# FFN layers in six full groups of 8 sequences and nine mixed tiles of 2, in place of ten groups, with a weight ring of four slots and resident gamma and beta

## The chip, the cores and the metric

The kernel runs on one core of one Trainium2 chip. The metric is the device time of one execution in microseconds, lower is better. The time before is the median of three runs.

## What is computed

Four layers over 64 sequences of 64 tokens and 512 features (float32). Layers 0, 2 and 3 are feed-forward layers whose weights are chosen per sequence by a role. The roles drawn are 1 or 2; the kernel has room for three. Layer 1 is attention with two wide feed-forward stages; the change doesn't touch its arithmetic.

```python
# x: [64, 64, 512]; role: [64]; W_down: [3, 512, 256]; W_up: [3, 256, 512]; gamma, beta: [3, 512]
def ffn(role, x, W_down, b_down, W_up, b_up, gamma, beta):
    h = gelu(einsum('bsh,bhk->bsk', x, W_down[role]) + b_down[role][:, None, :])
    y = x + einsum('bsk,bkh->bsh', h, W_up[role]) + b_up[role][:, None, :]
    yn = (y - mean(y)) * rsqrt(var(y) + 1e-5)
    return yn * gamma[role][:, None, :] + beta[role][:, None, :]

x = ffn(role, x, ...)          # layer 0
x = attention_and_mlps(x, ...) # layer 1
x = ffn(role, x, ...)          # layer 2
x = ffn(role, x, ...)          # layer 3
```

## The kernel before

**Grouping.** Sequences are sorted by role on the chip. A group holds 8 sequences of one role, that is 512 tokens or four tiles of 128. Each role starts a new group, so `NG` = 64 / 8 + 3 - 1 = 10 groups cover every possible mix of roles, and 16 of their 80 slots are empty (they are computed all the same). Class `Route` works out the slots: `dve_tables` (L176) is a chain of 49 small DVE steps, each waiting for the one before; PE's `pe_tables` and `pe_ranks` (L260, L270) turn them into row numbers, between the `fold` products (L1010, plain fp32) that prepare matrices for layer 1. POOL copies the numbers into one tile per group (`pool_rows`).

**Precision.** An FFN product is three fp32r matmuls: high x high, high x low, low x high (`product`, L57 to L59). ACT writes the high part (a Copy to fp32r), DVE the low part (a subtraction). This goes for weights (`act_split_down` L469, `dve_split_down` L519), transposed tokens (L486, L538) and hidden values (L497, L545).

**A group.** Class `Ffn` runs layer 0 as `first` (10 groups) and layers 2 and 3 together as `last` (20 groups, `NJ`). POOL gathers a group's rows (L626, one indirect DMA of 128 rows of 8 KB). PE transposes them (16 transposes of 128x128, L423), does the down product (24 matmuls of 512 columns, two banks), ACT the gelu and the split, then PE the up product (4 tiles x 7 matmuls of 512 columns, L455 to L459). DVE adds the residual (L551) and takes statistics (L555, L562), ACT turns them into moments (L504, L505), POOL takes the power -0.5 (L601, L603), ACT normalises (L511), POOL applies gamma (L611) and beta (L616) and scatters the rows (L639). Layer 3 takes its tokens from layer 2's tiles on chip.

**Order.** The order on each engine is written out by hand. On PE, in round j: down product of j, first up tile of j - 1, transposes of j + 1, the other three up tiles of j - 1. On DVE: weight split of j + 1, two hidden parts of j, residual, transposed half, residual, transposed half of j + 1, then statistics and residuals of j - 1. On POOL, in the first layer: gather j + 2, rstd of j - 2, gamma and beta of j - 3, scatter j - 3. ACT's normalisation of j - 2 stands before its transposed half of j + 1.

**Loads.** SP loads a group's down weights (512 KB) into one of two raw buffers `w_raw` when the split of the group two before is done, and gamma and beta (512 KB, broadcast to all partitions, `sp_load_gain` L400) into one of two buffers when the group two before has been shifted. All up weights of a layer stay on chip. The raw buffers are the same that layer 1 uses for its weights.

**Between the stages.** Layer 1 reads its tokens in quarters of 16 sequences from DRAM (`load_x`), once the scatters that hold them have landed. ACT waits for the scatters of groups whose tiles layer 1 overwrites (L1114 and L1124 are its first writes there). At the end the last three groups' gamma and beta are applied by DVE (L569, L572) while POOL does one half tile.

Of the kernel before, what the change touches and what calls it, by code (L numbers as in the profile page):

```python
# [16 lines left out]
F32 = mybir.dt.float32  # L17
# [34 lines left out]

def product(pe, out, terms):
# [29 lines left out]
class Route:  # L83


    ROLES_OUT = 5
    SLOT_OUT = 20
    ROLE_ROW = 26
    FIRST_ROWS = 29
    RANK_OUT = 36  # L90
    CODES_OUT = 39
    TABLES = 45
    ALL = 49

    def __init__(self, nc, ctx, consts, roles, codes, cb2, at, bank):
        self.consts, self.roles, self.codes, self.cb2 = consts, roles, codes, cb2
        tiles = Tiles(nc, at)
# [7 lines left out]
        self.up_i = tiles.new("up_i", [NSEQ, ROLES], I32)  # L105
        self.up_r = tiles.new("up_r", [NSEQ, ROLES], I32)
        self.base = tiles.new("base", [NSEQ, ROLES])
        self.packed = tiles.new("packed", [NSEQ, ROLES])
        self.place = tiles.new("place", [NSEQ, ROLES])
        self.placed = tiles.new("placed", [NSEQ, ROLES])  # L110
        self.slot = tiles.new("slot", [NSEQ, 1])
        self.slot_i = tiles.new("slot_i", [NSEQ, 1], I32)
        self.in_group_i = tiles.new("in_group_i", [NSEQ, 1], I32)
        self.in_group = tiles.new("in_group", [NSEQ, 1])
        self.group = tiles.new("group", [NSEQ, 1])
        self.seq_off = tiles.new("seq_off", [NSEQ, 1])
        self.value = tiles.new("value", [NSEQ, 1])
        self.rank = tiles.new("rank", [NSEQ, 1])
        self.rank_off = tiles.new("rank_off", [NSEQ, 1])
# [3 lines left out]
        self.iota_grp = tiles.new("iota_grp", [NSEQ, NG])  # L123
        self.at_group = tiles.new("at_group", [NSEQ, NG])
        self.rank_at_group = tiles.new("rank_at_group", [NSEQ, NG])
        self.slot_rows = tiles.new("slot_rows", [P, NG])
        self.rows = tiles.new("rows", [P, NG])
        self.rank_rows = tiles.new("rank_rows", [P, NG])
        self.live_rows = tiles.new("live_rows", [P, NG])
        self.past1 = tiles.new("past1", [1, NG])  # L130
        self.past2 = tiles.new("past2", [1, NG])
        self.role_at = tiles.new("role_at", [1, NG])
# [21 lines left out]
        self.coded = sem("coded")  # L154

    def pool_make(self, pool):
# [8 lines left out]
        pool.iota(self.iota_grp[:], pattern=[[GS, NG]], base=0, channel_multiplier=0, **exact).then_inc(made, 1)  # L165
# [3 lines left out]
        pool.iota(self.slot_rows[:], pattern=[[P, NG]], base=NROWS, channel_multiplier=1, **exact).then_inc(made, 1)  # L169
        pool.wait_ge(made, 10)  # L170
# [5 lines left out]
    def dve_tables(self, v, src_row):  # L176
        tab_src, tab_dst, tab_row, target_bias, _ = self.consts
# [7 lines left out]
        step(v.memset(self.base[:], 0.0))  # L185
        step(v.memset(self.packed[:], 0.0))
        v.wait_ge(self.made, 12)
# [8 lines left out]
        step(v.tensor_scalar(self.up_i[:], count, float(GS - 1), None, ALU.add))  # L196
        step(v.tensor_scalar(self.up_r[:], self.up_i[:], -GS, None, ALU.bitwise_and))
        step(v.tensor_copy(self.base[:, 1:2], self.up_r[:, 0:1]))
        step(v.tensor_tensor(self.base[:, 2:3], self.base[:, 1:2], self.up_r[:, 1:2], ALU.add))
        step(v.tensor_tensor(self.place[:], self.base[:], within, ALU.add))  # L200
# [9 lines left out]
        step(v.tensor_scalar(self.at_group[:], self.iota_grp[:], self.group[:], self.value[:], ALU.is_equal, ALU.mult))  # L210
        assert steps[0] == self.SLOT_OUT

        step(v.tensor_scalar(self.past1[:], self.iota_grp[0:1, :], self.base[0:1, 1:2], None, ALU.is_ge))
        step(v.tensor_scalar(self.past2[:], self.iota_grp[0:1, :], self.base[0:1, 2:3], None, ALU.is_ge))
        step(v.tensor_tensor(self.role_at[:], self.past1[:], self.past2[:], ALU.add))
        for layer in range(3):
            step(v.tensor_scalar(tab_row[:, layer * NG:(layer + 1) * NG], self.role_at[:],
                                 float(ROLES * layer), None, ALU.add))
        assert steps[0] == self.ROLE_ROW
        v.wait_ge(self.slots, 1)  # L220
        step(v.scalar_tensor_tensor(out=self.rows[:], in0=self.ps_slot[:, 0:NG], scalar=float(SROWS),
                                    in1=self.slot_rows[:], op0=ALU.mult, op1=ALU.add))
        for j in range(2):
            step(v.tensor_scalar(src_row[j][:], self.rows[:, j:j + 1], float(NROWS - 1), None, ALU.min))
        assert steps[0] == self.FIRST_ROWS

        step(v.tensor_copy(self.packed[:, 1:2], count[:, 0:1]))
        step(v.tensor_tensor(self.packed[:, 2:3], self.packed[:, 1:2], count[:, 1:2], ALU.add))
        step(v.tensor_tensor(self.place[:], self.packed[:], within, ALU.add))
# [1472 lines left out]
```

## Time and profile before

| | |
|---|---|
| three runs | 2487.82 us median (2485.74 to 2488.30) |
| profiled execution | 2487.73 us |
| its span | 2485.9 us, so 1.83 us lie around it |
| mean granted TensorE clock | 0.995 |
| first layer, layer 1, last two layers | to about 185 us, to about 2195 us, to 2485.9 us |
| DMA | 195.32 MB, mean 79 GB/s |
| landing of a 512 KB down-weight load, of a scatter, of a gather (page, median) | 4.5 us, 8.0 us, 9.5 us |

How to read it: times are microseconds from the start of the span unless marked ns. PE is TensorE's matmul row, PEld its weight loads, DVE VectorE, ACT ScalarE, POOL GpSimd, SP SyncE. Matmuls are pipelined: a row's length is the latency of one, and the pace is the distance of the starts. Plain fp32 products have two records each, fp32r products one. A row `PE L423 ... x16` merges sixteen in a row. Idle time of an engine that is not the bottleneck costs nothing.

### The profile page before, as it was taken

Reading aid. Unit: us, or ns where it says so; the run is one execution under the profiler, and the core shown is the slowest. Engines: PE = TensorE matmul, PEld = TensorE weight load, DVE = VectorE, ACT = ScalarE, POOL = GpSimd, SP = SyncE. Lnnn points to the kernel's source line nnn. Section 1 sums busy time; section 2 is a strip of 40 time slices with the busy share of each in tenths; the row PEclk is TensorE's granted clock in tenths of the full one; section 3 lists DMA queues with packets and bytes.
Section 4 is the critical chain, followed back from the end, with each engine's and each line's share of the span. In section 5 each row is a group of like instructions: output and inputs, shape, how many; then the busy total and the mean of one; then the engine's idle time right before and its main releaser. Section 6 shows DMA issues by size and latency. Waiting matters only on the chain.

```text
span 2485.9 us, 27593 instructions
## 1 busy us (share of the span) xinstructions
PE 2445.6 (98%) x11362; PEld 2032.5 (82%) x11362; DVE 1022.3 (41%) x1415; ACT 898.5 (36%) x1227; POOL 402.5 (16%) x312
## 2 busy tenths in 40 slices
PE   8999999999999999999999999999999999999996
PEld 5878888888888888888888888888888888888885
DVE  4774434222333343223243332233433422268776
ACT  4564423222334332223243322232432222346653
POOL 2786000000000000000000000000100000018886
PEclk9999999999999999999999999999999999999998
DMA  6463111210111112111111121102101211144243
GB/s 247 178 219 111 68 51 51 85 51 35 51 68 51 51 51 79 40 51 51 68 52 51 41 78 51 51 28 92 51 34 51 85 51 43 59 163 145 77 144 136
DMA packets 41521, 195.32 MB, mean 79 GB/s; under 512 B 5666, under 2 KB 5666, under 8 KB 24756
## 3 DMA queue, kind: packets, MB, share of 16 engines
q1 hardware_dynamic: 35636, 151.60, 18.0%
q0 software_dynamic: 5760, 41.95, 4.2%
q8 instruction: 91, 1.49, 0.2%
q14 instruction: 34, 0.28, 0.0%
HBM read 162.07 MB, written 31.46 MB: 78 GB/s over the span
## 4 chain that ended last, share of the span: by engine, by line
PE 97%; DVE 1%; DMA 1%; POOL 0%; issue 0%; ACT 0%; SPq 0%; DVEq 0%; ACTq 0%; POOLq 0%
PE pair L57 23%; PE pair L59 23%; PE pair L58 23%; PE pair L962 2%; PE pair L970 2%; PE pair L969 2%; PE pair L961 2%; PE pair L960 2%; PE pair L968 2%; PE pair L459 2%; PE pair L457 2%; PE pair L458 2%; PE pair L423 2%; PE pair L1010 1%; PE pair L937 1%; PE pair L921 1%
## 5 line engine op out<-in xcount | busy, mean ns | idle before, releaser
L1325 DVE TENSOR_TENSOR h_lo<-g,h_hi 128x512 fp32r<-128x512 f32 x256 | 179.1, 700 | 745.1 <-ACT h_hi L1149 744.8
L1147 ACT ACTIVATE g<-pair,bias_cols 128x512 f32<-128x512 f32 x256 | 176.5, 690 | 647.9 <-PE pair L59 411.5
L57 PE MATMUL pair<-h_hi,w_hiB 128*128 128x512 f32 x1024 | 399.0, 390 | 0.0
L59 PE MATMUL pair<-h_hi,w_loB 128*128 128x512 f32 x1024 | 398.4, 389 | 0.0
L58 PE MATMUL pair<-h_lo,w_hiB 128*128 128x512 f32 x1024 | 398.4, 389 | 0.0
L57 PE MATMUL pair<-o_hi,w_hiA 128*128 128x512 f32 x768 | 299.1, 390 | 0.0
L59 PE MATMUL pair<-o_hi,w_loA 128*128 128x512 f32 x768 | 298.8, 389 | 0.0
L58 PE MATMUL pair<-o_lo,w_hiA 128*128 128x512 f32 x768 | 298.7, 389 | 0.0
L1102 ACT ACTIVATE w_hiB<-w_raw 128x2048 fp32r<-128x2048 f32 x36 | 69.1, 1920 | 533.7 <-PE pair L59 504.9
L1537 POOL COPY acc<-xr 128x1024 f32<-128x1024 f32 x16 | 15.9, 1034 | 1357.8 <-PE pair L998 1349.7
L59 PEld LDWEIGHTS pair<-h_hi,w_loB 128*128 128x128 f32 x1024 | 192.2, 188 | 40.0
L58 PEld LDWEIGHTS pair<-h_lo,w_hiB 128*128 128x128 f32 x1024 | 192.3, 188 | 39.8
L57 PEld LDWEIGHTS pair<-h_hi,w_hiB 128*128 128x128 f32 x1024 | 192.2, 188 | 39.4
L59 PEld LDWEIGHTS pair<-o_hi,w_loA 128*128 128x128 f32 x768 | 144.2, 188 | 30.1
L58 PEld LDWEIGHTS pair<-o_lo,w_hiA 128*128 128x128 f32 x768 | 144.2, 188 | 29.8
L57 PEld LDWEIGHTS pair<-o_hi,w_hiA 128*128 128x128 f32 x768 | 144.2, 188 | 29.7
L1149 ACT ACTIVATE h_hi<-g 128x512 fp32r<-128x512 f32 x256 | 162.1, 633 | 8.1
L1332 DVE TENSOR_TENSOR x_tok<-pair,x_tok 128x512 f32<-128x512 f32 x128 | 86.8, 689 | 185.8 <-PE pair L59 185.8
L1332 DVE TENSOR_TENSOR acc<-pair,acc 128x512 f32<-128x512 f32 x128 | 86.0, 687 | 141.9 <-PE pair L59 141.9
L1279 DVE TENSOR_TENSOR w_loA<-w_raw,w_hiA 128x2048 fp32r<-128x2048 f32 x36 | 85.3, 2368 | 67.3 <-ACT w_hiA L1102 67.3
L1279 DVE TENSOR_TENSOR w_loB<-w_raw,w_hiB 128x2048 fp32r<-128x2048 f32 x36 | 84.6, 2350 | 49.1 <-ACT w_hiB L1102 49.1
L960 PE MATMUL pair<-o_hi,w_hiA 128*128 128x512 f32 x256 | 99.6, 389 | 0.0
(234 smaller groups left out, 4370.8 us busy)
## 6 DMA issues: line engine op xcount, KB each, us to landing
w_raw<-in_units_a SPq DMA_DIRECT2D x32, 1024.0 KB
w_raw<-in_units_b SPq DMA_DIRECT2D x32, 1024.0 KB, 4.8
w_raw<-in_units_c SPq DMA_DIRECT2D x16, 1024.0 KB, 4.8
w_raw<-in_w_packed SPq DMA_DIRECT2D x30, 512.0 KB, 4.5
w_raw<-in_rows_packed SPq DMA_DIRECT2D x20, 512.0 KB, 4.5
x<-stage SPq DMA_DIRECT2D x32, 256.0 KB, 2.1
x_tok<-x SPq DMA_DIRECT2D x12, 512.0 KB, 7.5
first_gain<-in_rows_packed SPq DMA_DIRECT2D x10, 512.0 KB, 4.6
```

Source lines behind the costliest of these rows:

```text
L57: pe.matmul(out, lh, rh, start=(i == 0), stop=False)
L58: pe.matmul(out, lh, rl, start=False, stop=False)
L59: last = pe.matmul(out, ll, rh, start=False, stop=(i == len(terms) - 1))
L423: last = pe.transpose(self.turned[i][:, t, k * P:(k + 1) * P], self.x[j % self.NX][:, i * self.HALF + t, k * P:(k + 1) * P], self.consts[4 ...
L457: pe.matmul(self.bank_U[t % 2], self.h_hi[u][:, k, ts], hi[k], start=False, stop=False)
L960: pe.matmul(bank[q], lh, rh, start=(i == 0), stop=False)
L1102: act.activation(w_hi[slot][:].rearrange("p k n -> p (k n)"), w_raw[i], ACT.Copy).then_inc(hi_done[slot], 1)
L1147: act.activation(g[q % 2][:], bank[q % 4], ACT.Gelu, bias=bias_at).then_inc(gelu_done, 1)
L1149: act.activation(h_hi[:, j, cols(n)], g[q % 2][:], ACT.Copy).then_inc(hhi_done, 1)
L1279: v.tensor_tensor(w_lo[slot][:].rearrange("p k n -> p (k n)"), w_raw[i], w_hi[slot][:].bitcast(F32).rearrange("p k n -> p (k n)"), ALU.sub ...
L1325: v.tensor_tensor(h_lo[:, j, cols(n)], g[q % 2][:], h_hi[:, j, cols(n)].bitcast(F32), ALU.subtract).then_inc(hlo_done, 1)
L1332: v.tensor_tensor(into[:, m, cols(n)], bank[4 + r % 4], into[:, m, cols(n)], ALU.add).then_inc(acc_done, 1)
```

## The change

The roles' full groups of 8 are kept, six of them, and every other sequence goes to a tile of two sequences (128 tokens) of one role. Nine such tiles cover every possible mix. Three of them, each with a role of its own, make a mixed job, so a layer is nine jobs, numbered from 0, in the order of `KINDS` (O a full group, M a mixed job), with 33 tiles of 128 tokens in place of 40.

- Mixed jobs: three down weights per job, one for each 128 columns; three gelus of 128 columns per bank; up weights, gamma and beta by tile; three gathers and three scatters of 128 rows of 2 KB.
- Weights: a ring of four slots, whose raw weights land in the place of the low parts and are subtracted in place. A load waits for the down product of the job that used the slot. On DVE and ACT the second and third split of a mixed job are put between the other steps.
- Gamma and beta of all three roles are loaded once per layer; the loads per group are gone. For the third layer they wait until layer 2's up weights are free.
- `dve_tables` has 75 steps in place of 49, with slots, ranks and row numbers for tiles as well.
- The fold matrices are loaded into the raw buffers after the last down product of the first layer (before: after the split of the last group).
- Buffers, and with them the scatters that layer 1 waits for, are placed anew; ACT also waits for the scatters of jobs 5 and 6 before its first values.

```diff
+KINDS = "OOOMOMOOM"
+NP = len(KINDS)
+OCT = KINDS.count("O")
+MT = 3
+MIXED = MT * KINDS.count("M")
+JOBS = tuple((kind == "O", KINDS[:p].count(kind) * (1 if kind == "O" else MT)) for p, kind in enumerate(KINDS))
+T_OF = tuple(GT if octet else MT for octet, _ in JOBS)
+UNITS = tuple((at,) if octet else tuple(OCT + at + i for i in range(MT)) for octet, at in JOBS)
...
-    ROLES_OUT = 5
-    SLOT_OUT = 20
...
-    ALL = 49
+    ROLES_OUT = 6
+    SLOT_OUT = 36
...
+    ALL = 75
...
+    def sp_load_down(self, sp, n):
+        j = self.job_of[n]
...
+        if n >= self.SLOTS:
+            sp.wait_ge(self.down_done, KB * (self.job_of[n - self.SLOTS] + 1))
...
-    def sp_load_gain(self, sp, j):
...
+    def sp_load_gain(self, sp, l):
+        for r in range(ROLES):
+            row = self.layers[l] * ROLES + r
+            sp.dma_start(self.gain[l][:, r, :],
+                         self.rows_packed[row:row + 1, 1:3, :].rearrange("r a n -> r (a n)").broadcast_to([P, 2 * D]))\
+              .then_inc(self.gain_in[l], 16)
...
+        spans = [slice(0, 512)] if octet else [slice(t * P, (t + 1) * P) for t in range(MT)]
         for m in parts:
             if m == 0:
                 pe.wait_ge(self.xlo_done, 2 * j + 2)
-                pe.wait_ge(self.wdlo_done, j + 1)
+                pe.wait_ge(self.wdlo_done, self.UB[j + 1])
...
-            product(pe, self.bank_D[m], [((self.wd_hi[u][:, k, ms], self.wd_lo[u][:, k, ms]),
-                                          (self.xT_hi[:, k, :], self.xT_lo[:, k, :])) for k in range(KD)])\
-                .then_inc(self.down_done, 1)
+            for u, ts in zip(units, spans):
+                last = product(pe, self.bank_D[m][:, ts],
+                               [((self.wd_hi[u][:, k, ms], self.wd_lo[u][:, k, ms]),
+                                 (self.xT_hi[:, k, ts], self.xT_lo[:, k, ts])) for k in range(KD)])
+            last.then_inc(self.down_done, 1)
...
+        for t, ts in enumerate(spans):
+            last = act.activation(self.bank_D[m][:, ts], self.bank_D[m][:, ts], ACT.Gelu,
...
+        else:
+            for t in range(MT):
+                pool.indirect_dma_start(out=self.x[j][:, t, :], out_offset=None, in_=self.src[1][0:TOKENS, :],
+                                        in_offset=bass.IndirectOffsetOnAxis(ap=self.src_rows[j][t][:], axis=0))\
+                    .then_inc(self.x_in[j % 2], 16)
...
+            sp.wait_ge(first.down_done, KB * NP)
+            for f in range(2):
+                sp.wait_ge(fold_stored[f], 16)
+                sp.dma_start(w_raw[f], (fold_m, fold_v)[f]).then_inc(raw_in[f], 16)
...
+            for i in range(2):
+                sp.wait_ge(end_stored[i], 8 * TT)
+            last.sp_load_gain(sp, 0)
...
-            for i in (3, 4):
-                act.wait_ge(first.stored[i], 16 * STORES.count(i))
+            for i in (1, 2, 3):
+                act.wait_ge(first.stored[i], first.stored_all(i))
...
+            for i in (4, 5):
+                act.wait_ge(first.stored[i], first.stored_all(i))
...
                 for m in range(KB):
                     last.dve_hidden(v, j, m)
+                if more:
+                    last.dve_split_down(v, last.units_from(j + 1, 1, 2))
                 last.dve_residual(v, j - 1, 0)
-                if j + 1 < last.NJ:
+                if more:
                     last.dve_transposed(v, j + 1, 0)
                 last.dve_residual(v, j - 1, 1)
-                if j + 1 < last.NJ:
+                if more:
                     last.dve_transposed(v, j + 1, 1)
+                    last.dve_split_down(v, last.units_from(j + 1, 2, 3))
```

## Rows read from the trace of the kernel before

**Rows 1.** Page, part 1: busy time, share of the span, instructions.
```profile
PE 2445.6 (98%) x11362; PEld 2032.5 (82%) x11362; DVE 1022.3 (41%) x1415; ACT 898.5 (36%) x1227; POOL 402.5 (16%) x312
```
**Rows 2.** Page, part 4: the chain that ended last, by engine.
```profile
PE 97%; DVE 1%; DMA 1%; POOL 0%; issue 0%; ACT 0%; SPq 0%; DVEq 0%; ACTq 0%; POOLq 0%
```
**Rows 3.** Chain in order of time (start, us, what): first and seventeenth transposes.
```profile
2220.02 1.75 PE pair L423 x16
...
2436.88 1.75 PE pair L423 x16
```
**Rows 4.** Timeline of PE (start, us, what): a down product's start, the next operation.
```profile
2239.94 0.39 PE L57 MATMUL pair<-last_xT_hi,last_wd_hi 128*128 128x512 f32 x1
...
2245.38 0.39 PE L455 MATMUL pair<-last_up_rows,last_pick 128*128 x1
```
**Rows 5.** Timelines of PE and PEld, then a window: PE, PEld, DVE, ACT, POOL busy, clock.
```profile
2246.97 1.91 PE L423 MATMUL pair<-ident,last_x 128*128 128x128 f32 x16
239.05 7.31 PE L937 MATMUL pair<-probsT,x_tok 128*128 128x128 f32 x64
246.09 0.19 PEld L57 LDWEIGHTS pair<-o_hi,w_hiA 128*128 128x128 f32 x1
246.20 0.19 PEld L58 LDWEIGHTS pair<-o_lo,w_hiA 128*128 128x128 f32 x1
29.09 7.03 PE L1010 MATMUL pair<-factor,factor 128*128 128x512 f32 x16
239.10:246.20 7.10, 7.10 (x67) 7.10 (x65) 4.50 (x6) 5.62 (x9) 0.00 (x0) 1.00 0.00 0
```
**Rows 6.** Timelines of DVE and PE in one steady group; in brackets the idle time.
```profile
2276.43 1.23 DVE L538 TENSOR_TENSOR last_xT_lo<-pair,last_xT_hi 128x1024 fp32r<-128x1024 f32 x1 [1.02 <-ACT last_xT_hi L486]
2278.23 1.21 DVE L538 TENSOR_TENSOR last_xT_lo<-pair,last_xT_hi 128x1024 fp32r<-128x1024 f32 x1
2280.60 0.39 PE L57 MATMUL pair<-last_xT_hi,last_wd_hi 128*128 128x512 f32 x1
2284.32 1.22 DVE L519 TENSOR_TENSOR last_wd_lo<-w_raw,last_wd_hi 128x1024 fp32r<-128x1024 f32 x1
```
**Rows 7.** Timeline of POOL in the first layer: one round and the next gather.
```profile
93.29 0.98 POOL L626 DMA_INDIRECT first_x<-in_x,first_src_row  x1 [0.30 <-issue]
...
95.71 4.73 POOL L611 TENSOR_TENSOR first_x<-first_x,first_gain 128x1024 f32<-128x1024 f32 x2
100.40 4.78 POOL L616 TENSOR_TENSOR first_x<-first_x,first_gain 128x1024 f32<-128x1024 f32 x2
105.47 1.05 POOL L639 DMA_INDIRECT x<-first_x,first_dst_row  x1 [0.29 <-POOL first_x L616]
106.83 0.97 POOL L626 DMA_INDIRECT first_x<-in_x,first_src_row  x1 [0.30 <-issue]
```
**Rows 8.** Timeline of PE at the start: slots, first fold, first transposes.
```profile
8.07 0.60 PE L268 MATMUL pair<-at_group,at_rows 64*128 64x10 f32 x2 [3.17 <-DVE at_group L210]
11.00 5.43 PE L1010 MATMUL pair<-factor,factor 128*128 128x512 f32 x8 [2.33 <-DMA factor<-in_wkT]
...
27.35 1.91 PE L423 MATMUL pair<-ident,first_x 128*128 128x128 f32 x16
```
**Rows 9.** Into layer 1: timeline of ACT and POOL, a stretch's clock, the chain.
```profile
169.01 0.60 ACT L1114 ACTIVATE xr<-pair 128x512 f32<-128x512 f32 x1 [3.46 <-DMA x<-first_x,first_dst_row]
202.13 0.58 ACT L1124 ACTIVATE x_tok<-pair 128x512 f32<-128x512 f32 x1
194.92 1.04 POOL L639 DMA_INDIRECT x<-first_x,first_dst_row  x1 [0.29 <-POOL first_x L616]
176.00:182.00 6.00, 4.71 (x15) 3.58 (x14) 4.52 (x9) 5.78 (x13) 0.13 (x1) 0.72 0.52 198
179.06 0.43 PE pair L457
```
**Rows 10.** Timeline of DVE near the end: gamma for the last group.
```profile
2472.45 2.50 DVE L569 TENSOR_TENSOR last_x<-last_x,w_raw 128x512 f32<-128x512 f32 x4 [0.55 <-DMA w_raw<-in_rows_packed]
```

More of the change, by code:

```diff
@@ L719, in program @@
-        routed = Route(nc, ctx, consts, roles, codes, cb2, where["probs"], bank)
-        assert routed.end <= where["probs"] + 3 * 4 * HT * P
-        folded_at = [first.x[5 + f][:].rearrange("p t n -> p (t n)") for f in range(2)]
+        routed = Route(nc, ctx, consts, roles, codes, cb2, tiles, where["probs"], bank)
+        assert routed.end <= where["probs"] + 3 * 4 * HT * P
+        oct_row, oct_rank = ([(row,) for row in rows] for rows in (routed.oct_row, routed.oct_rank))
+        tok_src, tok_rank, tok_live, tok_dst = (
+            {t: rows[t:t + MT] for t in range(0, MIXED, MT)} for rows in (routed.tok_src, routed.tok_rank, routed.tok_live, routed.tok_dst))
@@ new lines, in per_job, with both_rows @@
+        def per_job(octets, mixed):
+            return [octets[at] if octet else mixed[at] for octet, at in JOBS]
+        def both_rows(a):
+            return a, a.rearrange("a (t n) -> (a t) n", n=D)
+        half = 4 * KD * 512
+        six = 4 * MT * D
+        wd_lo = places["o_hi"] - 2 * half
+        assert wd_lo >= where_raw
+        first = Ffn(nc, ctx, "first", consts, routed, (0,), tiles, {
+            "x": (where["acc"], where["acc"] + half, where["xc_hi"], where["xc_hi"] + half, places["o_hi"],
+                  where["x_tok"], where["x_tok"] + half, places["first_c"], where["h_hi"]),
+            "xT": where["xc_lo"], "h": where["h_lo"], "wd_hi": where["w_hiA"], "wd_lo": wd_lo, "wu": (where["w_hiC"],),
+            "gain": (places["o_lo"],), "raw_rows": places["first_c"], "up_rows": where["h_hi"] + half,
+            "pick": where["h_hi"] + 2 * half - 2048},
+            pairs, both_rows(first_args["src"]), both_rows(first_args["dst"]), per_job(oct_row, tok_src), per_job(oct_rank, tok_rank),
+            first_args["w_packed"], first_args["rows_packed"], STORES)
@@ new lines, in program @@
+        o = places["o_hi"]
+        last = Ffn(nc, ctx, "last", consts, routed, (1, 2), tiles, {
+            "x": (where["x_tok"], where["x_tok"] + half, o, o + half, o + half + six, o + 2 * half + six,
+                  where["acc"], where["acc"] + half, o + 2 * half + 2 * six),
+            "xT": where["xc_hi"], "h": where["h_hi"], "wd_hi": where["xc_lo"], "wd_lo": wd_lo,
+            "wu": (where["w_hiA"], where["w_hiA"] + 8 * ROLES * KB * D), "gain": (where["h_lo"], where["w_hiA"]),
+            "raw_rows": where["probs"], "up_rows": o + 2 * half + 3 * six, "pick": where["expd"]},
+            pairs, both_rows(last_args["src"]), both_rows(last_args["dst"]), per_job(oct_rank, tok_live), per_job(oct_row, tok_dst),
+            last_args["w_packed"], last_args["rows_packed"], [p % 2 for p in range(NP)], first)
@@ L722, in program @@
+        assert o + 2 * half + 4 * six <= places["first_c"] + half
+        folded_at = [sb(f"folded{f}", [P, KD * D], at=where["x_tok"] + half * f) for f in range(2)]
         HIDDEN = HTILES * SB
@@ L851, in _ @@
             sp.wait_ge(lo_done["A"], NA * SB)
[L852 removed]
             sp.wait_ge(lo_done["B"], NBU * SB)
[L854 removed]
+            for n in range(2):
+                last.sp_load_down(sp, n)
             last.sp_load_rows(sp)
@@ L1020, in _ @@
             fold(1, range(2))
-            for j in range(NG):
+            for j in range(NP):
                 first.pe_down(pe, j)
@@ L1163, in _ @@
             act.wait_ge(bias_in, 16)
-            for j in range(NG):
-                role = first.role_of(act, j)
+            for j in range(NP):
+                roles = first.roles_of(act, j)
                 if j >= 2:
```

796 lines of the change are left out of this document (438 added, 358 removed).

## The prediction

> **What bounds the kernel now.** First the page: PE is busy 98% of the span, no other engine over half [rows 1]. A busy PE may still be one that others pace, so next the chain that ended last: 97% of it is PE [rows 2]. The chain in order of time then gives the measure of the stage that the change touches. From 2220.02 to 2436.88 us the transposes of sixteen successive groups come 216.86 us apart, 13.554 us a group, and PE has no wait between [rows 3]. The FFN layers are therefore priced in PE time, and only then does one ask who else could become late.
>
> A group on PE [rows 4]: its 24 down matmuls of 512 columns run from 2239.94 to 2245.38, 5.44 us, 226.7 ns each. (A row's own length, 0.39, is the latency of one; they overlap, so I price by start to start.) The up product has 4 tiles of 7 such matmuls, 28 x 226.7 = 6.35 us. The 16 transposes take what is left, 13.554 - 5.44 - 6.35 = 1.77 us. A layer is ten groups, 135.5 us; three layers, 406.6 us.
>
> **PE's work after.** A layer has six full groups, unchanged: 81.3 us. It has three mixed jobs of three 128-token tiles. Each has 12 transposes (1.32 us) and 3 tiles of up (21 x 226.7 = 4.76 us). The down product can no longer use one weight for 512 columns: each tile has its own, so it is 3 x 24 = 72 matmuls of 128 columns in place of 24 of 512. Columns fall from 512 to 384, instructions triple. The whole case hangs on the pace p of an fp32r matmul of 128 columns with its own weight load, and no such row exists; 3 x 3 x 72 = 648 of them are issued.
>
> Bounds for p. From below: if only columns and the fixed part counted, 226.7 ns for 512 is 213.3 of columns at 2.4 GHz and 13.4 fixed, so 53.3 + 13.4 = 67 ns. From nearby: every 128-column stream of this trace, each with its own weight load, goes at about one pace. The 16 transposes start within 1.91 - 0.27 = 1.64 us, 15 steps, 109 ns; the 64 plain fp32 matmuls of the attention need 7.31 - 0.28 = 7.03 for 63 steps, 112 ns [rows 5]. Two fp32r weight loads that had nothing to wait for start 0.11 us apart (246.09, 246.20) [rows 5]: the load can be had at that pace for this type too. From above: plain fp32 needs two records per product, and a 512-column record takes (7.03 - 0.62)/15 = 427 ns, so a product costs 854 ns, four times the columns. If an fp32r matmul this narrow were run like plain fp32, it would cost 2 x 112 = 223 ns [rows 5]. I take 111 ns, by the transposes and the two loads, and keep 67 and 223 for the range.
>
> Mixed job: 4.76 + 1.32 + 72 x 0.111 = 14.07 us, so slightly more than a full group for three quarters of its tokens. Layer: 81.3 + 42.2 = 123.5 us, 12.0 less. Three layers: -36.0 us.
>
> A rule of the Trainium skill prices this otherwise. "TensorE: Matmul & The Clock Gate", section "Back-to-back issue gap", gives about 81 ns for a stream of 128-column load and matmul pairs. By it the estimate would be 648 x 30 ns = 19 us better than mine. No 4-byte stream here comes under 109 ns, so the trace speaks against it for this type.
>
> **What newly stops PE between jobs.** Before a down product PE waits for DVE's last part of the transposed tokens. In a steady group DVE starts that part at 2278.23, ends it at 2279.44, and PE begins the down product at 2280.60: 1.16 us of slack [rows 6]. The change puts two more weight splits in front on DVE for a mixed job, one before the residuals, one behind the last transposed part. A split is 1.2 us long [rows 6].
> - Jobs 3 and 8 (mixed, behind full ones): the earlier split fits in DVE's idle 1.02 us, the later one eats the slack of 1.16: about 0.2 us each.
> - Job 5 (mixed, two behind mixed job 3): between its transposes and its down product PE has two output tiles of job 3 in place of three, 1.59 us less cover, its own transposes are 0.44 shorter, and the late split adds 1.2; its last part is half as long, -0.6. 1.59 + 0.44 + 1.2 - 0.6 - 1.16 = 1.5, and with the earlier split and the hops between queues 2.
> - Jobs 7 and 10 (full, two behind a mixed one): 1.59 - 1.16 = 0.4.
> - The up tiles that wait for a residual pushed back by a split: 0.5, twice a layer.
> That is 3.5 us a layer, +11 in all; bounds 4 (all of it but job 5's stall fits into jitter) and 25 (every mixed job stalls by 2.8).
>
> POOL is the next suspect: in the first layer it goes round in 13.55 us without rest, gather 1.0, gain and shift 9.4, scatter 1.1, and the rest small operations and 0.3 of issue twice [rows 7]. A mixed job gives it three gathers and three scatters of 1.3 us, +5.3 in all, and takes a quarter of the 9.4, -2.4. The round in which it prepares job 8 and finishes job 3 becomes 16.5 us against 12 of PE; but the layer as a whole has 33 tiles in place of 40, and the rounds ahead leave it some 3 us. What waits for it is ACT's normalisation, which stands ahead of ACT's transposed parts; I count nothing, and up to 6 us in the bound above. In the last two layers gathers and scatters fall into different layers and POOL has rest. ACT's three gelus of 128 columns in place of one are hidden under 6 us of other PE work.
>
> The ring: with four slots a load of 512 KB (4.5 us to land by the page) is issued when the job four units back has left PE, at least one whole job ahead of its use. Nothing. Resident gamma and beta remove twenty-odd loads of 512 KB that nobody but the last two jobs waited for: nothing in the middle.
>
> **The edges.** Start: DVE's table steps come one after another, 15 of them in the 3.17 us that PE waits for the slots, 0.21 each [rows 8], and there are 26 more, 5.5 us. PE stands behind them twice. The slots are 16 steps later, at 11.4 instead of 8.07, and the fold behind them waits for its DMA until 11.00 anyway. The ranks (25 steps later) come near 16.6, when that first fold ends (11.00 + 5.43). The tables must end before PE needs them at 27.35, and do by 6 us [rows 8]. +0.5; bounds 0 and 4 (the folds no longer cover).
> Into the attention: today ACT waits 3.46 us until a scatter has landed, and part of the stretch behind it has a granted clock of 0.72 [rows 9]. After, the same position in the pipeline is scattered (job 4, two rounds before the last), so the wait stays. The fold matrices are now loaded only after the last down product, 5 us before ACT's split asks for them. One scatter more (job 6) must land before ACT copies the first values; at its place POOL today issues a scatter at 194.92, and ACT copies at 202.13 [rows 9], so with a landing of 8 us (the page's median) ACT would be 1 us late, with a whole query product of PE's beside it. +1; bounds 0 and +8.
> Into the last layers: SP waits for the final stores (2 us to land) and issues 1.5 MB of gamma and beta ahead of the second up weights. +1; bounds 0 and +6, when the third and fourth job's weights come late.
> Tail: DVE ends with gains and shifts for ten tiles; one tile less is two operations of 0.61, and the 0.55 us for the last gain load is gone [rows 10]. Against it, the last job has three scatters of 1.3 in place of one [rows 7]. -1; bounds -2 and +2.
>
> **Sum.** 2485.9 - 36.0 + 11 + 0.5 + 1 + 1 - 1 = 2462.4 us of span. The profiled execution took 1.83 us more than its span, and is 0.09 from the median. Forecast 2464.2 us, 0.9% faster. Its own range: p from 109 to 125 ns is -1 to +9, stalls -7 to +14, edges -4 to +16, not all at once: 2452 to 2480.
>
> **Rivals.**
> 1. Narrow fp32r matmuls run four passes, as plain fp32 does. Then p is 223 ns, 648 x 112 = +73 us: 2537 us, slower by 2%. For it: the only 128-column matmuls that multiply here are plain fp32, and the fp32r gain is seen at 512 columns alone. Against it: nothing in the trace links passes to width; 512 and 128 columns of plain fp32 both take two passes a record. It decides from p = 111 + 23.6/0.648 = 147 ns. Chance 0.26. "FP8 and Floating Point Precision", section "TensorE Precision Notes", of the Trainium skill lists four passes for true fp32 and a truncated read for reduced precision, and ties neither to a width; the 854 ns agree with the four.
> 2. The clock falls while the array is half idle for 8 us. The matmuls behind it then go 0.43 us apart instead of 0.227, as at 179.06, inside the stretch with 0.72 [rows 9]. If all 21 up matmuls of nine mixed jobs did, 9 x 21 x 0.2 = +38: 2502 us. Against it: 7.1 us of 128-column stream at 1.00 [rows 5]. Chance 0.05. The skill's "TensorE: Matmul & The Clock Gate", section "Why this matters for your kernels", warns of thin matmuls for this reason and would pad them instead, which is what the kernel before does.
> 3. The cover does not hold: DVE's splits, POOL's sixteen-us round or the late ring loads stall every job at its down product, 27 x 1 us more: 2491 us, within 0.2%. Chance 0.05.
> 4. Loads overlap better, p near 67 ns: 648 x 44 = -28 us, and 4 us more of stalls as covers shrink: 2440 us. Chance 0.06.
> The number of mixed tiles is fixed in the program (15 units whatever the roles), so that PE's work shrinks as stated is certain.
>
> **How the numbers follow.** Forecast 0.58, rivals 0.26, 0.05, 0.05, 0.06. A measurement of this kernel can tell about 0.2%, 5 us. Faster: 0.58 + 0.06 = 0.64. Same: the third, 0.04 after rounding. Slower: 0.26 + 0.05 + 0.01 = 0.32. Fast cases alone hold too little, so the range must reach the first rival: 2450 to 2545, which leaves out rival 4 and some tails.
>
> **What would show it.** Right: 128-column fp32r starts 0.11 us apart in the down product of a mixed job; transposes of two full jobs still 13.55 apart; a wait of about 2 us at job 5 on DVE's weight split, repeated in each layer; the first layer 12 us shorter. Wrong: starts 0.22 apart there (rival 1), a granted clock below 1 behind mixed jobs (2), waits on POOL or DMA at many jobs (3), starts under 0.1 (4).

## The result, and the profile after

The changed kernel takes 2535.97 us (median of four, 2530.98 to 2536.74) beside 2487.45 for the kernel before: a ratio of 1.0192, interval 1.018 to 1.0204. It is 1.9% slower, where 0.9% faster was forecast. The profiled execution took 2530.98 us, the shortest of the four, with a span of 2528.9, so 43.0 us more than the span before. The other three have a mean granted clock of 0.975 beside its 0.977 and are 4.6 to 5.8 us longer; that is about what one more down product at half clock would cost (below), but they were not traced. In what follows L71 to L73 are the down product's matmuls, L523 the transposes, L561 to L565 the up product, L631 DVE's split of a down weight, L651 its last part of the transposed tokens, L665 the residual, L726 and L732 POOL's gain and shift.

The page, part 1, beside [rows 1]: PE is busy 12 us longer though it has less to do, and 71 us of the span are not PE's, 40 before.

```profile
PE 2457.6 (97%) x11493; PEld 2049.7 (81%) x11493; DVE 1023.6 (40%) x1379; ACT 884.1 (35%) x1233; POOL 388.0 (15%) x338
```

The stretches in which the mixed jobs' down products run, eight of the nine (columns: stretch, length, busy PE, PEld, DVE, ACT, POOL, granted clock, DMA share, GB/s). All have the same 72 matmuls.

```profile
78.60:86.67 8.07, 8.07 (x74) 8.07 (x73) 5.42 (x12) 1.85 (x7) 2.91 (x3) 1.00 0.57 207
112.03:127.42 15.39, 15.39 (x73) 15.39 (x73) 4.16 (x9) 1.74 (x6) 13.21 (x9) 0.50 0.38 137
166.77:180.13 13.36, 13.36 (x72) 13.36 (x73) 4.32 (x11) 1.74 (x6) 9.60 (x9) 0.58 0.19 80
2273.78:2288.04 14.26, 14.26 (x72) 14.26 (x73) 4.17 (x9) 1.74 (x6) 11.35 (x7) 0.54 0.22 74
2327.53:2340.99 13.46, 13.46 (x72) 13.46 (x73) 5.42 (x12) 1.75 (x6) 7.41 (x7) 0.58 0.00 0
2391.71:2399.78 8.07, 8.07 (x73) 8.07 (x73) 5.42 (x12) 1.75 (x6) 4.16 (x4) 1.00 0.01 2
2425.12:2440.41 15.29, 15.29 (x72) 15.29 (x73) 4.17 (x9) 1.74 (x6) 12.11 (x8) 0.50 0.17 70
2480.44:2488.51 8.07, 8.07 (x73) 8.07 (x73) 4.32 (x11) 1.74 (x6) 4.44 (x4) 1.00 0.32 133
```

At full clock the product takes 8.07 us, the forecast's 72 x 0.111 = 8.0. In five of nine jobs the mean granted clock is 0.50 to 0.58, so most or all of the time is at the lower level of 1.2 GHz, and the same work takes 13.4 to 15.4. One of these jobs, job 8 of the second layer (timeline of PE), starts at full clock and loses it after 2 us:

```profile
2328.00 0.28 PE L72 MATMUL pair<-last_xT_lo,last_wd_hi 128*128 128x128 f32 x1
2328.11 0.28 PE L73 MATMUL pair<-last_xT_hi,last_wd_lo 128*128 128x128 f32 x1
...
2330.33 0.41 PE L72 MATMUL pair<-last_xT_lo,last_wd_hi 128*128 128x128 f32 x1
2330.54 0.41 PE L73 MATMUL pair<-last_xT_hi,last_wd_lo 128*128 128x128 f32 x1
...
2341.53 0.63 PE L563 MATMUL pair<-last_wu_hi,last_h_hi 128*128 x1
2341.95 0.63 PE L564 MATMUL pair<-last_wu_lo,last_h_hi 128*128 x1
```

Starts are 0.11 apart, then 0.21, and the up matmuls behind are 0.42 apart in place of 0.227, as in [rows 9].

What stands ahead of that job is the second half of the loss. The chain in order of time (start, length, what):

```profile
2318.84 2.90 DVE last_wd_lo L631
2321.74 0.61 DVE last_x L665
...
2322.39 0.50 PE pair L561
...
2326.00 1.53 issue
2327.53 0.30 PE pair L71
```

A weight split of 2.90 us holds the residual back, and the residual an up tile of PE; the next split then ends only with PE's start of the down product. DVE and POOL in the same microseconds (timelines):

```profile
2314.27 1.22 DVE L631 TENSOR_TENSOR last_wd_lo<-last_wd_raw,last_wd_hi 128x1024 fp32r<-128x1024 f32 x1
2318.84 2.90 DVE L631 TENSOR_TENSOR last_wd_lo<-last_wd_raw,last_wd_hi 128x1024 fp32r<-128x1024 f32 x1 [0.25 <-ACT last_wd_hi L574]
2324.59 2.84 DVE L631 TENSOR_TENSOR last_wd_lo<-last_wd_raw,last_wd_hi 128x1024 fp32r<-128x1024 f32 x1
2315.89 4.76 POOL L726 TENSOR_TENSOR last_x<-last_x,last_gain 128x1024 f32<-128x1024 f32 x2 [0.36 <-issue]
2320.60 5.75 POOL L732 TENSOR_TENSOR last_x<-last_x,last_gain 128x1024 f32<-128x1024 f32 x2
```

The split at 2314.27, in POOL's quiet time, takes 1.22 us; the two that overlap POOL's gain and shift take 2.90 and 2.84, and POOL's shift 5.75 for two in place of 4.76. The up stretch from 2319.11 to 2327.53 is 8.42 us long where its 21 matmuls need 4.76: a stall of 3.6. Against the pure work (4.76 for 21 matmuls, 3.17 for 14) such stretches are 5.6 to 5.7 us too long at job 5 of each layer, 3.6 to 3.7 at job 8, 0.9 to 2.0 at job 3 and 0.6 at job 7: 10.9 us in each of the first two layers, 11.8 in the third.

Where the 43.0 us are: start +0.9, first layer from its first down product to the end of its last +15.3, from there to the last layers' first down product -2.7, the last two layers +26.3, tail +3.2. By cause: PE's work at full clock -35 (forecast -36); stalls between jobs +32 (forecast +11); half clock +40, of which 31.4 in five down products (71.8 us in place of 5 x 8.07), 6.6 in the up tile behind each and 2 in transposes (forecast 0); start, entry and tail +1.4; the remaining 5 us are small pieces that stay unexplained. The stalls alone would have brought this execution to some 2491 us, no faster than before.

### The profile page after: what moved, and what is told of

Same layout as the page of the kernel before. It is cut to its first block, busy times and chain, and to the rows that moved or that the text cites. A ratio compares the mean times of both kernels' runs of the same rounds, so it can differ in the third digit from the quotient of the medians.

```text
span 2528.9 us, 28083 instructions
## 1 busy us (share of the span) xinstructions
PE 2457.6 (97%) x11493; PEld 2049.7 (81%) x11493; DVE 1023.6 (40%) x1379; ACT 884.1 (35%) x1233; POOL 388.0 (15%) x338
## 4 chain that ended last, share of the span: by engine, by line
PE 94%; DVE 3%; ACT 1%; issue 1%; DVEq 0%; DMA 0%; POOL 0%; ACTq 0%
PE pair L71 23%; PE pair L72 23%; PE pair L73 23%; PE pair L1118 2%; PE pair L1111 2%; PE pair L1110 2%; PE pair L1119 2%; PE pair L1120 2%; PE pair L1112 2%; PE pair L563 1%; PE pair L564 1%; PE pair L565 1%; PE pair L1160 1%; PE pair L1087 1%; PE pair L1071 1%
## 5 line engine op out<-in xcount | busy, mean ns | idle before, releaser
L71 PE MATMUL pair<-h_hi,w_hiB 128*128 128x512 f32 x1024 | 399.0, 390 | 0.0
L73 PE MATMUL pair<-h_hi,w_loB 128*128 128x512 f32 x1024 | 398.4, 389 | 0.0
L71 PE MATMUL pair<-o_hi,w_hiA 128*128 128x512 f32 x768 | 299.1, 390 | 0.0
L73 PE MATMUL pair<-o_hi,w_loA 128*128 128x512 f32 x768 | 298.8, 389 | 0.0
L73 PEld LDWEIGHTS pair<-h_hi,w_loB 128*128 128x128 f32 x1024 | 192.2, 188 | 39.9
L71 PEld LDWEIGHTS pair<-h_hi,w_hiB 128*128 128x128 f32 x1024 | 192.2, 188 | 39.8
L71 PEld LDWEIGHTS pair<-o_hi,w_hiA 128*128 128x128 f32 x768 | 144.2, 188 | 29.9
L73 PEld LDWEIGHTS pair<-o_hi,w_loA 128*128 128x128 f32 x768 | 144.1, 188 | 29.9
```

## The experiments

**Theory A.** A split of DVE beside POOL's gain and shift is slow; that makes the stalls; a stall and a weight-bound narrow stream together halve the clock. Rivals: B, the narrow stream does it alone; C, the split is slow by itself; D, the stall alone does it. e2 to e7 were executed once each, so their main readings are lengths and granted clocks inside one trace and not small differences of the whole time.

**e1_splits_early.** In ACT and DVE, for `first` and `last` alike (abridged, as the edits below are):

```
 (ACT, at the end of round j)
-  act_split_down(units_from(j + 2, 0, 1))      # and (j+1, 1, 2), (j+1, 2, 3) later in the round
+  act_split_down(units_from(j + 2, 0, 3))
 (DVE, at the start of round j)
-  dve_split_down(units_from(j + 1, 0, 1))      # and (j+1, 1, 2), (j+1, 2, 3) later in the round
+  dve_split_down(units_from(j + 1, 0, 3))
```

> All weight splits of a mixed job are moved to where DVE starts its round (ACT makes the high parts at the end of the round before), in GpSimd's quiet time; nothing is left out. Theory A (the late splits run beside GpSimd's gain and shift operations, take 2.8 to 3.4 us instead of 1.2, hold back DVE's last part of the transposed tokens, and the stall of 4 to 6 us ahead of the narrow stream is what lets the clock fall): splits of 1.2 to 1.3 us, stalls ahead of the mixed down products under 1.5 us each, granted clock 1.00 in all nine of them at 8.07 us each, 2455 to 2475 us in all. Rival B (the narrow weight-bound stream drops the clock by itself, the stall only stands beside it): the stalls go (-25 us), but down products of 13 to 15 us stay in about five of nine jobs: 2495 to 2515 us. Rival C (a split is slow for its own operands, not for GpSimd): splits of 2.8 us at the new place as well, no gain: 2525 us or more.

2473.73 us, ratio to the kernel before 0.9944 (0.9928 to 0.9961). Moving ten-odd lines of queue order turned 1.9% slower into 0.6% faster, 62 us. All nine mixed down products are at full clock, 7.98 to 8.10 us long; one of them:

```profile
105.54:113.63 8.09, 8.09 (x72) 8.09 (x73) 5.90 (x9) 2.27 (x7) 7.47 (x5) 1.00 0.16 68
```

B is refuted: the same stream, no drop. The cure is partial, though. Five of the 45 splits still start inside a POOL operation and take 2.1 to 3.4 us (the mean of all is 1.39). Two of them lead to stalls of 1.6 and 1.8 us ahead of mixed down products, where under 1.5 was expected; the clock held. And PE still waits 3.4 us at job 7 of the first layer; the clock falls there too, and that down product takes 7.16 us in place of 5.44. POOL's timeline shows why PE waits:

```profile
126.98 0.99 POOL L746 DMA_INDIRECT first_x<-in_x,tok_src  x1 [0.30 <-issue]
...
129.55 0.96 POOL L746 DMA_INDIRECT first_x<-in_x,tok_src  x1 [0.30 <-issue]
130.53 1.04 POOL L711 TENSOR_TENSOR columns<-columns 128x4 f32<-128x4 f32 x1
```

Three gathers for job 8 stand ahead of the small rstd operation, for which ACT's normalisation waits, in front of its transposed parts.

**e2_pool_narrow.** Every operation stays in its place; POOL's gain and shift cover 16 columns of 512; the other columns of the output go without gamma and beta.

```
-  x[:, ts, :] ... gain[..., 0:D]       (mult; add likewise)
+  x[:, ts, 0:16] ... gain[..., 0:16]
```

> The changed kernel with GpSimd's gain and shift on 16 of 512 columns (the other columns of the output go without gamma and beta); order and place of every other operation as in the changed kernel. Theory A: no split of DVE over 1.3 us though all stand where they stood; stall ahead of the mixed down products at most 2.5 us (job 5) and else under 1; granted clock 1.00; 2450 to 2475 us. Rival B: the stalls go, five of nine mixed down products still at half clock, 2495 to 2515 us. Rival C: splits stay at 2.8 us and the time at 2530 us.

2491.18 us. The view of one line, first in the changed kernel, then here (minimum, median, maximum in ns):

```profile
L631 DVE TENSOR_TENSOR last_wd_lo<-last_wd_raw,last_wd_hi x30: 1183/1216/3329, 2179.8 to 2477.5; 128x1024 fp32r<-128x1024 f32 x30
```

```profile
L631 DVE TENSOR_TENSOR last_wd_lo<-last_wd_raw,last_wd_hi x30: 1189/1215/1226, 2165.9 to 2442.9; 128x1024 fp32r<-128x1024 f32 x30
```

So POOL is the cause of the slow splits; C is refuted. The stalls are close to what the forecast had thought: about 2.5 us at job 5 (forecast 2), 1.0 at jobs 3 and 8 (0.2, and 0.5 for the up tile). But the time missed the expected 2450 to 2475: all three job 5 still ran at half clock, behind a stall of only 2.5 us, the third for 13.16 us (columns as above):

```profile
108.44:122.12 13.68, 13.68 (x73) 13.68 (x73) 4.17 (x9) 1.84 (x7) 3.44 (x7) 0.57 0.25 103
2256.74:2271.63 14.89, 14.89 (x73) 14.89 (x73) 4.17 (x9) 1.84 (x7) 2.37 (x6) 0.52 0.01 6
```

**e3_one_weight** and **e4_two_spans.** The stalls stay, the stream behind them gets wider; some tiles get another tile's down weight.

```
-  spans = ... [slice(t * P, (t + 1) * P) for t in range(MT)]
+  spans = ... [slice(0, MT * P)]                                  (e3)
+  spans = ... [slice(0, 2 * P), slice(2 * P, 3 * P)]              (e4)
```

> The changed kernel with the first of a mixed job's three weights used for all 384 columns: 24 matmuls of 384 columns in place of 72 of 128 (the second and third tile get the first one's down weight, their own are still loaded and split). The stalls ahead of it stay. Theory A, in the form that stall and narrow stream are needed together: granted clock 1.00 behind the same stalls of 4 to 6 us, a down product of 24 x 0.17 = 4.1 us, so -36 us for the work and -40 us for the clock: 2455 to 2475 us. Rival D (the stall alone drops the clock, whatever comes behind it): granted clock about 0.5 to 0.6 in the five jobs, down products of 6 to 8 us and up matmuls 0.43 us apart behind them: 2480 to 2500 us.

> The changed kernel with the down product of a mixed job in two spans, 256 columns on the first weight and 128 on the second (the second tile gets the first one's weight, the third tile the second one's). It prices one matmul of 256 columns and shows what paces the 128-column stream. If the weight load paces it (0.11 us a load at full clock, the columns beneath it free): a 256-column matmul costs 0.11 to 0.12 us, 48 matmuls 5.4 us. If narrow matmuls of this type carry a second pass: 0.21 us for 256 columns, 7.8 us. On the clock it stands between the kernel with 72 and that with 24 matmuls; theory A says that jobs behind a stall of 4 to 6 us are the only candidates for less than 1.00.

2475.52 and 2477.16 us. e3 behind a stall, in slices of 2 us (columns as above):

```profile
106.00:108.00 2.00, 0.00 (x0) 0.00 (x0) 2.00 (x1) 1.12 (x2) 2.00 (x2) 1.00 0.00 0
108.00:110.00 2.00, 0.90 (x3) 0.93 (x4) 2.00 (x3) 0.00 (x0) 2.00 (x1) 0.55 0.00 0
110.00:112.00 2.00, 2.00 (x8) 2.00 (x7) 2.00 (x7) 0.30 (x2) 1.71 (x2) 0.50 0.00 0
112.00:114.00 2.00, 2.00 (x7) 2.00 (x7) 0.78 (x1) 0.67 (x4) 1.68 (x3) 0.50 0.46 197
114.00:116.00 2.00, 2.00 (x10) 2.00 (x10) 0.56 (x1) 0.77 (x3) 1.06 (x3) 0.75 1.03 365
116.00:118.00 2.00, 2.00 (x12) 1.64 (x11) 0.22 (x1) 1.60 (x5) 2.00 (x1) 1.00 0.84 279
```

Theory A in its first form is wrong: the clock falls behind the stall without a narrow stream too. But here it is back before the up product, and that down product takes 6.97 us in place of 4.24, a loss of 2.7 and not of 7. Of the five mixed jobs of e3 behind a stall of over 3 us, three lost part of their clock (6.97, 5.57 and 5.09 us) and two none; rival D had expected five at 0.5 to 0.6 and slow up matmuls behind, and 2480 us or more. This gave theory A2: the stall lowers the clock, the stream behind it decides for how long.

e4 gives the pace of three widths together with e3 (timeline of PE, first of e4):

```profile
2223.11 0.28 PE L73 MATMUL pair<-last_xT_hi,last_wd_lo 128*128 128x256 f32 x1
2223.23 0.28 PE L71 MATMUL pair<-last_xT_hi,last_wd_hi 128*128 128x256 f32 x1
...
2224.48 0.27 PE L73 MATMUL pair<-last_xT_hi,last_wd_lo 128*128 128x128 f32 x1
2224.59 0.27 PE L71 MATMUL pair<-last_xT_hi,last_wd_hi 128*128 128x128 f32 x1
```

```profile
2226.89 0.34 PE L73 MATMUL pair<-last_xT_hi,last_wd_lo 128*128 128x384 f32 x1
2227.07 0.33 PE L71 MATMUL pair<-last_xT_hi,last_wd_hi 128*128 128x384 f32 x1
```

From the first of these starts on, ten steps of 256 columns cost 0.119 us each; 128 columns cost 0.111, four steps of 384 cost 0.175 each, and 512 cost 0.227. So the second 128 columns are nearly free, and it is not the columns that pace the 128-column stream. That p was 0.111 is confirmed. The weight load is what fits: PEld is busy without a break in that stream, and the two loads of [rows 5] start 0.11 apart. Every matmul of these kernels has a load of its own, though, so a fixed cost of each pair is not told apart from it.

In e4, too, three of the six mixed jobs behind a stall of over 3 us lost part of their clock (7.04, 7.10 and 8.68 us in place of 5.58), and all had it back before the up product.

**e5_stall_full, e6_early_stall4, e7_early_stall2.** To e1, a stall was added by letting DVE make the last transposed part again, ahead of full jobs (e5) or of the mixed ones (e6, e7):

```
+  if i == 1 and j % NP in (4, 6, 7):        # e5;  (3, 5, 8) in e6 and e7
+      for _ in range(4):                    # 4 in e5 and e6, 2 in e7
+          <the same subtraction into xT_lo>;  wait for it
```

> The kernel with the early splits, and a stall put ahead of the down products of full jobs 4, 6 and 7 of each layer: DVE makes the last transposed part five times instead of once (four repeats of 1.2 us; nothing is left out). PE then waits 3 to 4.5 us more there, nine times, ahead of a stream of 512 columns. Theory A2 (a stall of some 4 us halves the granted clock by itself; a stream of 512 columns gets it back within 3 to 6 us, a stream of 128 columns does not until it has ended): 9 x 4 = 36 us of stalls and at each about 2 us more for the down product (7 in place of 5.44 us), full clock again before the up product: 2473.7 + 36 + 16 = 2525 us, 2515 to 2535. Theory A in its first form (the stall harms only a narrow stream): clock 1.00, down products of 5.44 us, 2510 us or less.

> The same four repeats of DVE's last transposed part, now ahead of the mixed jobs 3, 5 and 8 of each layer (repeats of 0.6 us for these, since a mixed job's second part is one tile), so PE waits 1.5 to 2.5 us more at each of nine places, ahead of the 128-column stream. Theory A2 with a stall of about 2 us as in the kernel with 16 columns on GpSimd: half clock for the whole stream (13 to 15 us in place of 8) where the stall comes near 2.5 us, above all at job 5; if all nine fall: +9 x (2 + 6.5) = 76 us, 2550 us; if the three of job 5 alone: 2473.7 + 18 + 20 = 2512 us. Rival B2 (a short stall does nothing, the clock fell in that kernel for another reason): clock 1.00 everywhere, 2495 us or less.

> Two repeats instead of four ahead of the mixed jobs, 0.6 us each: stalls of 0.5 to 1.5 us. Theory A2: too short to bring the clock down, 2473.7 + 9 x 1 = 2483 us, all nine mixed down products at 8 us. Rival B3 (the narrow stream is on the edge and any stall tips it): at least four of nine at 13 us or more, 2500 us and over.

Measured: 2516.15, 2542.46 and 2478.04 us. In e5 nine stalls of about 4 to 5 us stand ahead of 512-column streams. Eight of nine down products have a lower mean clock and take 7.1 to 8.3 us in place of 5.4 or 5.6, one is untouched, and each up product behind is at 1.00. Three of them:

```profile
98.27:105.34 7.07, 7.07 (x24) 5.69 (x25) 7.07 (x13) 1.65 (x4) 2.09 (x3) 0.78 0.51 167
2399.61:2407.90 8.29, 8.29 (x24) 6.58 (x25) 7.78 (x14) 1.65 (x4) 3.30 (x3) 0.65 0.01 2
2434.55:2440.13 5.58, 5.58 (x25) 4.62 (x25) 4.94 (x12) 1.53 (x4) 1.20 (x1) 1.00 0.00 0
```

In e6 stalls of 1.6 to 4.6 us stand ahead of the 128-column streams, and seven of nine stay at half clock to their end:

```profile
80.44:94.13 13.69, 13.69 (x72) 13.69 (x73) 5.46 (x12) 1.74 (x6) 8.50 (x5) 0.57 0.29 112
2492.33:2500.43 8.10, 8.10 (x73) 8.10 (x73) 4.36 (x11) 1.74 (x6) 4.39 (x4) 1.00 0.32 132
```

A2 stands: the stalls were put in and nothing else was changed, and behind them the wide streams lost up to 3 us, the narrow ones 5 to 7. Both times lie within what was expected: e5 at the low end of 2515 to 2535, e6 between 2512 for three drops and 2550 for nine. e7, with mostly under 1.5 us of stall, lost 4 us against e1 and no whole stream.

The 72 mixed down products of the eight kernels that keep 72 matmuls (the changed one, e1, e2, and e5 to e9), sorted by the stall in the up stretch ahead (its length less the 4.9 us, or 3.6 for two tiles, of the undisturbed ones):

| stall ahead | products | at half clock throughout |
|---|---|---|
| under 1.55 us | 46 | 0 |
| 1.55 to 3.2 us | 17 | 8 |
| over 3.2 us | 9 | 7 (one more for under 1 us) |

In the middle row all eight drops have the gap directly ahead of the down product (e2, e6), and three more with such a gap kept the clock; where up tiles stand between the longest gap and the down product (the changed kernel, e1, e8, e9, one of e7), none fell. That is a tendency in few cases, not tested by itself. Nor is it shown why one of two like stalls lowers the clock and the other does not.

**e8_pool_order** and **e9_landed_first.** These test the remaining stalls, which e1 had shown, and look for a version that beats both kernels.

```
 (POOL, round j; e8)
+  rstd_shift(j - 2)                     # now ahead of the gathers
   gather(j + 2)
-  rstd_shift(j - 2)
+  scatter(j - 4) if that job is mixed   # held back by one round
   gain_shift(j - 3); scatter(j - 3) if not mixed
 (tail; e8) DVE alone does gain and shift of the last three jobs; POOL: rstd ahead of scatters
 (e9) of the first layer only job 3 is held back; UP_SPLITS = (3, 5, 6) -> (4, 5, 7)
 (SP, after the last down product; e9)
+  for i in (1, 2, 3): sp.wait_ge(first.stored[i], first.stored_all(i))
   for f in range(2): <1 MB load of the fold matrices>
```

> Early splits, and GpSimd's queue put in another order: the small rstd and shift operations ahead of a mixed job's three gathers, a mixed job's three scatters behind the next ones; at the tail DVE alone does gain and shift of the last three jobs, and the last job is scattered tile by tile. Nothing is left out. Theory: GpSimd's six queued gathers and scatters of 1.3 us made ACT's normalisation late, and that PE (3.4 us and 1.7 us of lower clock ahead of job 7, 1.6 ahead of job 8 in the first layer), and at the tail they held back the last normalisation: minus 6 to 7 us in the first layer, minus 3 to 4 us at the tail, in all 2462 to 2466 us. Rival: the waits move to the gathers themselves or to the entry into the attention, and under 2 us are gained: 2472 us.

e8 took 2477.55 us, ratio 0.9963 (0.9949 to 0.9977): 4 us worse than e1 and 5.5 above the rival's 2472; the rival's case, and more. The stall at job 7 is gone and the tail is 3 us shorter, as expected, but the time came back at the entry into the attention. ACT's timeline there:

```profile
168.30 0.60 ACT L1265 ACTIVATE xr<-pair 128x512 f32<-128x512 f32 x1 [9.53 <-DMA x<-first_x,oct_rank]
```

The scatter was issued at 157.01. The first layer's last down product comes 4.6 us sooner than in e1, so that the two megabyte loads that are issued behind it now started together with this scatter, which landed after 11 us. In e1 the scatter went ahead of them and landed in 4.6. And job 5's scatters, held behind an rstd that came only at 181, made the attention wait 2.6 us.

> The kernel before this one with three edits, nothing left out: SyncE waits until the scatters that the attention needs have landed before it issues the attention's megabyte loads (behind the last down product they overtook the fourth job's scatter, which then landed 11 us after its issue and held PE 7 us); job 5's scatters of the first layer go out at once again (held back, they made the attention wait 2.6 us and more); the second layer's up weights are split in rounds 4, 5 and 7 instead of 3, 5 and 6, so never just ahead of a mixed job's three splits (2.3 us of PE at the second layer's job 8). Theory: 6 to 7 us at the entry, 6 in the attention, 2 in the last layers come back: 2477.5 less 12 to 15, so 2462 to 2466 us, with the granted clock 1.00 in all mixed down products. Rival (the entry's wait has another cause than the loads): 2468 to 2474 us.

e9: 2465.86 us, ratio 0.9910 (0.9896 to 0.9924), within the expected 2462 to 2466. The entry now waits 2.40 us for that scatter, and all mixed down products are at 1.00:

```profile
165.46 0.60 ACT L1267 ACTIVATE xr<-pair 128x512 f32<-128x512 f32 x1 [2.40 <-DMA x<-first_x,oct_rank]
```

## Why the prediction was wrong, point by point

Two terms of the sum failed. The stalls were put at +11 us and came to +32, because "a split is 1.2 us long" does not hold beside POOL. The clock was put at nothing, with a rival of 0.05, and cost +40. With both as forecast the kernel would have been faster. The measured 2536 lies within the stated 2450 to 2545 and 1 us from rival 1's 2537, but that is coincidence: the range was drawn out to a rival whose mechanism did not happen.

**PE's work and its pace: right.** p was put at 0.111, measured 0.111 to 0.112; PE's work fell by 35 us against the forecast's 36. The first rival, four passes, did not happen. The mechanism that the chosen value implied, that the weight load paces the stream, fits 256 columns at 0.119.

**The stalls: right in kind and place, mis-sized.** Job 5 was to stall by 2 us, jobs 3 and 8 by 0.2 with 0.5 for an up tile, 3.5 us a layer in all (the items as listed add to 3.8). It was 5.7 at job 5, 0.9 to 2.0 at job 3 and 3.6 at job 8; 10.9 to 11.8 a layer. The failed term is "a split is 1.2 us long": its row lay in POOL's quiet time [rows 6], and the change put further splits beside POOL's gain and shift. e2 gives the size of the error: with POOL's operations shrunk, the same queue order stalls by 2.5 us at job 5 and 1.0 at jobs 3 and 8.

The trace of before had the warning: at its tail two DVE operations on SBUF tiles took 2.58 us at 2463.29 beside POOL's shift, and four of the same took 2.48 at 2467.00 without it. The Trainium skill says it outright: "SBUF — State Buffer", section "Who interferes with whom", has a DVE instruction with two SBUF inputs contend with a GpSimd instruction that reads SBUF, and calls the port pair that they share an exclusive lock. The traces agree. All 14 splits of the changed kernel that start while POOL's gain or shift runs end 1.08 us after that operation has ended, and so take 1.9 to 3.4 us in place of 1.2. The one at 2318.84 starts with 1.83 us of POOL's operation still to go and takes 2.90. Where the split starts first, POOL is the one that waits: in e1 a split at 2242.99 keeps its 1.22 us, and the gain that POOL begins 0.69 us later takes 2.77 in place of 2.40. L651, which reads one operand from PSUM, keeps its 1.2 beside POOL.

**POOL "counted at nothing": wrong in e1's light.** What the prediction named, POOL's queue ahead of ACT's normalisation, is real: three gathers cost PE 3.4 us at job 7 of the first layer. In the changed kernel the bigger stalls before it hide this, so it cost little there. It appeared when they were gone.

**Rival 2, the clock: the right object, wrong trigger and wrong price.** It had 0.05 and +38 us for "nine jobs, all 21 up matmuls at 0.43", caused by the half-idle array. Measured are +40, by luck: five jobs, most of it in the narrow stream itself, whose pace doubles to 0.213 and which the rival had priced at nothing. Its trigger was wrong: with less than 1.55 us of stall ahead the narrow stream never lowered the clock (46 of 46), and 7.1 us at 1.00 in [rows 5] was good evidence for that and no more. In these runs the clock fell with stalls. The trace of before showed that as well, in the stretch I quoted from [rows 9]. Its slices of 2 us:

```profile
174.00:176.00 2.00, 1.02 (x10) 0.79 (x8) 2.00 (x4) 2.00 (x2) 0.00 (x0) 1.00 0.88 193
176.00:178.00 2.00, 0.71 (x5) 0.44 (x4) 2.00 (x7) 2.00 (x6) 0.00 (x0) 1.00 0.98 348
178.00:180.00 2.00, 2.00 (x7) 1.59 (x6) 1.23 (x1) 2.00 (x6) 0.00 (x0) 0.59 0.58 246
```

PE works 1.7 of 4 us, and then 0.59. I read the 0.72 as a price and did not ask what PE had done before it. Two terms were thus treated as independent that are one: a stall of a few microseconds costs itself, and the clock of what stands behind it. The Trainium skill has the rule in "TensorE: Matmul & The Clock Gate", section "Why this matters for your kernels", which says to avoid idle gaps between bursts of matmuls; the runs agree, and add what the gap costs by the stream behind it.

**Rival 3, waits at many jobs.** 27 x 1 us was its price; 32 us of stalls came, most of it in two jobs of each layer rather than in all. By themselves these stalls give the rival's 2491 us; the clock's 40 us came on top.

**Edges.** Start +0.9 (forecast +0.5). From the first layer's last down product to the first of the last two layers -2.7 (forecast +2 for both entries, lower bound 0, missed): the wait of 3.46 us for a scatter, which the forecast kept, is gone, since the late first layer gave the scatter time; e8 shows the danger that the forecast had put at +8. Tail +3.2 (forecast -1, bounds -2 to +2, missed): POOL's three scatters, put at 1.3 us each, stood ahead of the last rstd operations, and DVE's gains met POOL's (two took 5.05 us). e9 mends both, and its tail is still 1.1 us longer than the one before.

**The forecast of 2464.2** is within 2 us of the kernel with its queues mended (e9). The arithmetic of PE held; the assumption that its neighbours could feed it did not. That the two times are so near is in part luck: against the kernel before, e9's layers are 21.8 us shorter (forecast 25), the way between them 1.8 shorter (forecast 2 longer), the start 2.0 and the tail 1.1 longer (forecast 0.5 longer and 1 shorter).

## What to carry to other kernels

Price a moved or added operation by the place it lands in, not by the row where it stands today: here a DVE operation of 1.2 us that reads two SBUF tiles took 1.9 to 3.4 us when it started inside a GpSimd operation that reads SBUF. Before narrowing matmuls, look for gaps of over 1.5 us ahead of them. In these runs a gap cost its own length and, where the clock fell, 1.6 to 2.9 us more with a 512-column stream behind it, and 5 to 7 us more, plus 1 to 2 behind, with a 128-column stream of 8 us. And when a large change moves the time the wrong way, try the order of the queues before giving it up.

## What the runs showed of the hardware

- An fp32r matmul with its own weight load costs 0.111, 0.119, 0.175 and 0.227 us for 128, 256, 384 and 512 columns at full clock, and 0.213 and 0.42 for 128 and 512 at half.
- The granted clock came back 2 to 6 us into streams of 384 or 512 columns (e1, e3, e5). In 15 of 16 cases in which it fell ahead of a 128-column stream or within its first microseconds, it did not come back in the 13 to 15 us of the stream; the one exception (e7) had fallen over 2 us ahead of it. Why a stream that keeps PE busy without a break does not bring it back was not tested.
- A DVE subtraction with both inputs in SBUF that starts inside a GpSimd gain or shift (2.4 us) ends 1.08 us after it; one that starts first keeps its 1.2 us, and GpSimd's operation gets longer.
- One indirect scatter of 1 MB landed 4.6 us after issue when no load was issued with it (e1; 4.5 in e9), and 11.1 us after issue when two loads of 1 MB were issued within 0.7 us of it (e8).
